# Host-side weight layouts, mask products for the diagonal blocks, eight-group moment steps and unrolled loops in a recommender tower

## The chip, the cores and the metric

One core of one Trainium2 chip runs the whole kernel. The time is device microseconds of that core for one execution. TensorE is written PE (PEld for its weight loads), VectorE DVE, ScalarE ACT, GpSimd POOL, SyncE SP. A measurement of this kernel can tell about one per cent from no change.

## The reference, cut to what matters

The batch is 512 samples. For each, 26 rows of 32 values are gathered, one from each of 26 embedding tables, by a column of `ids`. Two layers of a compressed interaction network follow, and then a small network of three dense layers.

```python
def _cin_layer(x_prev, x0, W, b):
    return jnp.einsum('bik,bjk,hij->bhk', x_prev, x0, W) + b[None, :, None]
...
e = jnp.stack([tbl_0[ids[:, 0]], ..., tbl_25[ids[:, 25]]], axis=1)     # 512 x 26 x 32
x1 = _cin_layer(e, e, W1, b1)                                          # 512 x 128 x 32
x2 = _cin_layer(x1, e, W2, b2)
z = jnp.sum(jnp.concatenate([x1, x2], axis=1), axis=-1)                # 512 x 256
h = jnp.concatenate([z, dense_ctx], axis=1)
h = jnp.maximum(h @ W_top1 + b_top1, 0.0)                              # 512
h = jnp.maximum(h @ W_top2 + b_top2, 0.0)                              # 256
y = h @ W_top3
```

Only sums over the last axis (k) are needed, so the kernel forms products of pairs of fields, multiplies them with the fields over k on TensorE ("moments": every pair with every field, and with a column of ones), and multiplies the moments with weights that are folded from W1 and W2 at the start.

## The kernel before, in words

**Tiles.** The batch is worked in four tiles of 128 samples. Within a tile the 128 samples are 32 groups of 4, and a group's 4 x 32 values of k lie on the 128 partitions.

**Gathers.** POOL issues one indirect DMA for each field and tile, 104 in all (line 242). The fields come in three parts, of 13, 10 and 3 (`PARTS`). There is one buffer `rows` for all tiles: the gathers of part p of tile t+1 wait until part p of tile t has been transposed (`s_turn[p]`). POOL's loop runs twice over two tiles.

**VectorE in a tile.** `half_a` waits until the moments of the tile before are done, transposes part 0 (`fields_in`, line 616) and forms the products of its pairs (`products_a`, lines 771 to 777, 14 instructions). `half_b` transposes parts 1 and 2. `steps` then forms the remaining products four groups at a time (`products_b`, line 788, 8 instructions) and between them copies a few rows of the moments out of PSUM (line 650, four copies for each step).

**ScalarE in a tile.** `fill_diag` (line 467) copies the transposed fields into four diagonal blocks of `diag`, four copies for each part, for the next tile; `copy_moments` takes the moments out of PSUM in eight steps (lines 485 to 489); then come the copies of the first layer's two halves (`z`, lines 495 and 499), and the two dense layers' activations (504, 509) and the output row (514).

**TensorE in a tile.** `moments` (lines 321 and 322) runs 32 groups in eight steps of four, with two pairs of PSUM banks in turn: a step waits for its products and for the evictions of the step two before. The first part of tile t needs `diag` complete. After it come the second dense layer of tile t-1, the sums over the moments (lines 332 to 349) and the first dense layer of tile t.

**Setup.** W1 and W2 are loaded as they are. W2 is transposed on TensorE (line 275) and evicted by ACT (432), W1's pair sums are formed by DVE in small steps (570 to 598), the two are multiplied (281, 287), and DVE adds the parts of `folded` (662). A part of these additions and of the transposes of `folded` stands between the steps of tile 0.

Tiles 1 to 3 run in hardware loops on POOL, PE, ACT and DVE (ACT's covers tiles 1 and 2).

## Time and profile before

| | |
|---|---|
| time, median of 3 runs | 189.18 us (188.01 to 190.05) |
| span of the profiled execution | 269.0 us |
| POOL, gathers | 108.7 us busy, 104 instructions |
| PE, matmuls | 171.1 us busy |
| DVE | 94.1 us busy |
| ACT | 103.7 us busy |

The profiled execution's span is 79.8 us longer than the median of the runs. The profiled execution's own time outside the profiler is not among the times, so its span is all there is of it. The prediction has to say what that difference is.

### The profile page before, as it was taken

Reading aid. Unit: us, or ns where it says so; the run is one execution under the profiler, and the core shown is the slowest. Engines: PE = TensorE matmul, PEld = TensorE weight load, DVE = VectorE, ACT = ScalarE, POOL = GpSimd, SP = SyncE. Lnnn points to the kernel's source line nnn. Section 1 sums busy time; section 2 is a strip of 40 time slices with the busy share of each in tenths; the row PEclk is TensorE's granted clock in tenths of the full one; section 3 lists DMA queues with packets and bytes.
Section 4 is the critical chain, followed back from the end, with each engine's and each line's share of the span. In section 5 each row is a group of like instructions: output and inputs, shape, how many; then the busy total and the mean of one; then the engine's idle time right before and its main releaser. Section 6 shows DMA issues by size and latency. Waiting matters only on the chain.

```text
span 269.0 us, 3544 instructions
## 1 busy us (share of the span) xinstructions
PE 171.1 (64%) x1239; PEld 158.7 (59%) x1239; DVE 94.1 (35%) x370; ACT 103.7 (39%) x267; POOL 109.4 (41%) x110
## 2 busy tenths in 40 slices
PE   7900594209929388986300799954001999899997
PEld 7800583209729287976300789954002999888985
DVE  0576003210943086920000568500003569047200
ACT  1020330019595165494000462951003463966313
POOL 3778777720077400577774003877770000000000
PEclk9975598556997869996555599995555799999999
DMA  6700011000001000011000000001000000000000
GB/s 240 250 12 13 12 14 14 13 7 0 0 10 17 11 1 4 2 12 15 14 12 10 0 0 2 11 12 15 12 12 2 0 0 0 0 0 0 0 0 3
DMA packets 5729, 5.08 MB, mean 19 GB/s; under 512 B 2875, under 2 KB 5061, under 8 KB 5718
## 3 DMA queue, kind: packets, MB, share of 16 engines
q0 software_dynamic: 3328, 1.71, 4.7%
q1 hardware_dynamic: 1698, 2.34, 2.6%
q10 hardware_dynamic: 692, 0.89, 1.0%
q8 instruction: 6, 0.10, 0.2%
q14 instruction: 5, 0.04, 0.1%
HBM read 4.93 MB, written 0.00 MB: 18 GB/s over the span
## 4 chain that ended last, share of the span: by engine, by line
PE 35%; another core or an unknown queue 30%; ACT 15%; DVE 9%; issue 9%; POOL 0%; DVEq 0%; ACTq 0%; POOLq 0%
PE bank L321 9%; ACT diag L467 8%; PE bank L287 4%; DVE t L650 4%; PE bank L322 4%; PE bank L281 4%; PE bank L256 3%; PE bank L332 2%; DVE prod L771 2%; PE bank L372 1%; ACT w2t L432 1%; ACT t L486 1%; DVE prod L616 1%; PE bank L275 1%
## 5 line engine op out<-in xcount | busy, mean ns | idle before, releaser
L242 POOL DMA_INDIRECT rows<-in_tbl_dram,idx x104 | 108.7, 1045 | 91.1 <-DVE prod L616 57.4
L321 PE MATMUL bank<-diag,prod 128*128 128x108 f32 x256 | 60.7, 336 | 56.0 <-DVE t L650 44.3
L321 PEld LDWEIGHTS bank<-diag,prod 128*128 128x128 f32 x256 | 46.6, 227 | 59.5 <-issue 59.5
L650 DVE COPY t<-bank 13x64 f32<-13x64 f32 (+2 forms) x128 | 26.7, 209 | 108.6 <-ACT t L487 66.7
L322 PE MATMUL bank<-diag,prod 128*77 128x64 f32 x256 | 41.7, 249 | 0.3 <-issue 0.3
L322 PEld LDWEIGHTS bank<-diag,prod 128*77 128x77 f32 x256 | 36.8, 173 | 0.5 <-issue 0.5
L485 ACT COPY t<-bank 55x128 f32<-55x128 f32 x32 | 8.3, 259 | 71.9 <-remote 47.8
L467 ACT COPY diag<-prod 32x416 f32<-32x416 f32 (+2 forms) x48 | 33.4, 696 | 1.0
L287 PE MATMUL bank<-w1ab,w2t 128*128 128x169 f32 x52 | 16.0, 489 | 14.6 <-ACT folded L434 9.7
L287 PEld LDWEIGHTS bank<-w1ab,w2t 128*128 128x128 f32 x52 | 12.8, 278 | 17.5 <-ACT folded L434 10.4
L281 PE MATMUL bank<-w1s,w2t 128*128 128x183 f32 x52 | 10.8, 377 | 16.4 <-ACT w2t L432 15.6
L281 PEld LDWEIGHTS bank<-w1s,w2t 128*128 128x128 f32 x52 | 10.3, 233 | 16.9 <-ACT w2t L432 15.8
L788 DVE TENSOR_TENSOR prod<-prod 128x364 f32<-128x364 f32 x32 | 16.5, 536 | 0.8
L489 ACT COPY t<-bank 128x432 f32<-128x432 f32 x32 | 16.4, 512 | 0.0
L434 ACT COPY folded<-bank 128x366 f32<-128x366 f32 x13 | 5.8, 469 | 25.8 <-remote 11.7
L662 DVE TENSOR_TENSOR folded<-folded 128x6 f32<-128x6 f32 (+15 forms) x44 | 5.1, 177 | 27.4 <-ACT folded L434 13.2
L662 DVE TENSOR_TENSOR folded<-folded,ct 128x52 f32<-128x52 f32 (+13 forms) x51 | 11.6, 301 | 7.4 <-ACT ct L437 7.3
L349 PE MATMUL bank<-t,v 128*128 128x128 f32 x104 | 12.7, 279 | 0.0
L332 PE MATMUL bank<-t,v 128*128 128x128 f32 x104 | 12.4, 276 | 0.3 <-ACT t L489 0.3
L332 PEld LDWEIGHTS bank<-t,v 128*128 128x128 f32 x104 | 11.9, 192 | 0.6 <-ACT t L489 0.6
L349 PEld LDWEIGHTS bank<-t,v 128*128 128x128 f32 x104 | 11.9, 192 | 0.5
L363 PE MATMUL bank<-z,wt 128*128 128x128 f32 x64 | 9.0, 286 | 2.8 <-issue 2.1
(79 smaller groups left out, 186.3 us busy)
## 6 DMA issues: line engine op xcount, KB each, us to landing
rows<-in_tbl_dram,idx POOLq DMA_INDIRECT x104
wt<-in_W_top_dram SPq DMA_DIRECT2D x2, 512.0 KB
w<-in_L_rec_W_dram ACTq DMA_DIRECT2D x1, 832.0 KB
w<-in_L_rec_W_dram SPq DMA_DIRECT2D x1, 832.0 KB
w<-in_L_rec_W_dram SPq DMA_DIRECT2D x1, 338.0 KB
idx<-in_ids_dram SPq DMA_DIRECT2D x4, 13.0 KB
vec<-in_L_rec_b_dram ACTq DMA_DIRECT2D x2, 0.5 KB
dctx<-in_dense_ctx_dram ACTq DMA_DIRECT2D x1, 32.0 KB
```

Of the source, the lines that this page charges most:

```text
L242: pool.indirect_dma_start(rows[:, f, :], None, tables[f], bass.IndirectOffsetOnAxis(ap=idx[i][:, f:f + 1], axis=0)).then_inc(s_got[part], 16)
L281: mm = nc.tensor.matmul(ps[:, i * PAIRS:(i + 1) * PAIRS], w2t[:, x0 + i, :], w1s[:], start=True, stop=True)
L287: mm = nc.tensor.matmul(ps[:, i * HALF * HALF:(i + 1) * HALF * HALF], w2t[:, lo + x0 + i, :], rhs, start=True, stop=True)
L321: nc.tensor.matmul(m0[:, g * P:g * P + JW * QUADS], prod[:, G, 0:P], mov, start=True, stop=True)
L322: mm = nc.tensor.matmul(m1[0:M1, g * J1 * QUADS:(g + 1) * J1 * QUADS], prod[:, G, P:P + M1], mov[:, JLOW * QUADS:], start=True, stop=True)
L332: nc.tensor.matmul(Z2[:, 0:P], v0[:, j, :], t0[:, j, :], start=j == HALF, stop=False)
L349: mm = nc.tensor.matmul(Z2[:, 0:P], v0[:, j, :], t0[:, j, :], start=False, stop=j == HALF - 1)
L467: nc.scalar.copy(diag[q, :, f0:f1, r], prod[q, :, col:col + f1 - f0]).then_inc(s_diag, 1)
L489: nc.scalar.copy(dst(t0, 0, P, slice(0, JW)), view(m0, P, slice(0, JW), P)).then_inc(s_e0, 1)
L650: ins = nc.vector.tensor_copy(t1[p0:p0 + HALF, GRAM + slot:GRAM + slot + nb, n].rearrange("p j (g r) -> p j g r", r=QUADS), m1[64:64 + HAL ...
L662: ins = nc.vector.tensor_tensor(dest, dest, term[second], ALU.add)
L788: return eng.tensor_tensor(dst, left, right, ALU.mult)
```

## The change

- **Weights laid out by the host.** The host only reorders and concatenates: W1's two triangles come as two planes `w1p` whose sum is the pair sums, W2 comes transposed (`w2t`), the weights of the first sum come as two planes `w1t`, the vectors as columns, and the dense context transposed and in the order of the groups. The additions stay on the chip: one for `w1s`, one for `z1w`. TensorE's transposes of W2 and of the rest, and their evictions, are gone.
- **Diagonal blocks by mask products.** `fill_diag` on ACT is gone. `fields_in` on DVE multiplies the transposed fields, repeated four times, with a mask `quad` of ones and zeros: one `tensor_tensor` for each part.
- **Moment steps of eight groups.** Four steps for a tile, each with three PSUM banks, two sets in turn; one DVE copy or ACT copy of the small parts covers eight groups, the large one is two copies for each step. `products_b` stays at four groups, but its eight instructions stand in a row, ahead of the copies out of PSUM (`bands`).
- **A row buffer for each tile.** `rows[t]` with semaphores of their own; no gather waits for a transpose.
- **Loops written out.** No hardware loop is left on any engine.
- **Order.** The setup ends before the moments of tile 0 begin; in a tile the sums of `z2` stand ahead of `z1`, and the second dense layer uses one bank and one semaphore.

```diff
-            def fill_diag(t, parts):
-                act.wait_ge(s_mom, t * STEPS + STEPS)
-                for part in parts:
-                    f0, f1, col = PARTS[part]
-                    act.wait_ge(s_turn[part], t + 2)
-                    for r in range(QUADS):
-                        q = slice(32 * r, 32 * r + 32)
-                        nc.scalar.copy(diag[q, :, f0:f1, r], prod[q, :, col:col + f1 - f0]).then_inc(s_diag, 1)
...
             def fields_in(t, part):
                 f0, f1, col = PARTS[part]
-                dve.wait_ge(s_got[part], (t + 1) * (16 * (f1 - f0)))
-                nc.vector.transpose(prod[:, :, col:col + f1 - f0].rearrange("p g f -> p f g"),
-                                    rows[:, f0:f1, :]).then_inc(s_turn[part], 1)
+                n = f1 - f0
+                dve.wait_ge(s_got[t][part], 16 * n)
+                nc.vector.transpose(prod[:, :, col:col + n].rearrange("p g f -> p f g"),
+                                    rows[t][:, f0:f1, :]).then_inc(s_turn[part], 1)
+                dve.wait_ge(s_turn[part], t + 1)
+                nc.vector.tensor_tensor(diag[:, :, f0:f1, :],
+                                        with_dims(prod[:, 0, col:col + 1], (PCOLS, GROUPS), (1, n), (0, QUADS)),
+                                        with_dims(quad[:, 0:1], (0, GROUPS), (0, n), (1, QUADS)), ALU.mult)
...
-            with nc.gpsimd.Fori(0, TILES // 2) as u:
-                for i in range(2):
-                    pool.wait_ge(s_idx[i], u * 16 + 16)
-                    for part, (f0, f1, _) in enumerate(PARTS):
-                        pool.wait_ge(s_turn[part], u * 2 + i + 1)
+            for t in range(TILES):
+                if t < 2:
+                    pool.wait_ge(s_idx[t], 16)
+                for part, (f0, f1, _) in enumerate(PARTS):
...
-                for s in range(STEPS + 2):
-                    if s < STEPS:
-                        products_b(nc.vector, prod, s * GSTEP, GSTEP).then_inc(s_pb, 1)
-                    if between and 2 <= s < STEPS:
-                        add(*between[s - 2])
-                    if s >= 2:
-                        m1 = MOM[s % 2][1]
...
+                for s in range(PRODS):
+                    products_b(nc.vector, prod, s * GPROD, GPROD).then_inc(s_pb, 1)
+
+            def bands(t):
+                if t:
+                    dve.wait_ge(s_z1, t)
+                for s in range(STEPS):
+                    m1 = bank[3 * (s % 2) + 2]
+                    dve.wait_ge(s_mom, t * STEPS + s + 1)
```

How the instructions stand. DVE at the start of a tile after the first, before: L616 transposes part 0 out of `rows`, L771 are the pair products.

```order
L615 ISA [waits s_mom]
L616 STREAM_TRANSPOSE prod<-rows 128x13x32 [waits s_got0]
L622 REGISTER_ALU
L771 TENSOR_TENSOR prod<-prod 128x32x5 [waits s_turn0]
L771 TENSOR_TENSOR prod<-prod 128x32x4
L771 TENSOR_TENSOR prod<-prod 128x32x3
```

The same place in the changed kernel, tile 1:

```order
L447 STREAM_TRANSPOSE prod<-rows 128x13x32 [waits s_got1_0,s_mom]
L450 TENSOR_TENSOR diag<-prod,quad 128x32x52 [waits s_turn0]
L599 TENSOR_TENSOR prod<-prod 128x32x5
L599 TENSOR_TENSOR prod<-prod 128x32x4
L599 TENSOR_TENSOR prod<-prod 128x32x3
```

A product with 1,664 elements on each partition, with two inputs in SBUF, has come in directly ahead of the 14 products.

DVE from part 1 to the second step's copies, before:

```order
L616 STREAM_TRANSPOSE prod<-rows 128x10x32 [waits s_got1]
L628 COPY prod<-prod 128x32x6 [waits s_turn1]
L615 REGISTER_ALU
L616 STREAM_TRANSPOSE prod<-rows 128x3x32 [waits s_got2]
L788 TENSOR_TENSOR prod<-prod 128x4x91 [waits s_dup,s_turn2]
L788 TENSOR_TENSOR prod<-prod 128x4x91 x2
L644 REGISTER_ALU
L645 REGISTER_ALU [waits s_mom]
L647 ISA [waits s_e1]
L650 COPY t<-bank 13x4x16 [waits s_z]
```

And in the changed kernel:

```order
L447 STREAM_TRANSPOSE prod<-rows 128x10x32 [waits s_got1_1]
L450 TENSOR_TENSOR diag<-prod,quad 128x32x40 [waits s_turn1]
L462 COPY prod<-prod 128x32x6
L447 STREAM_TRANSPOSE prod<-rows 128x3x32 [waits s_got1_2]
L450 TENSOR_TENSOR diag<-prod,quad 128x32x12 [waits s_turn2]
L616 TENSOR_TENSOR prod<-prod 128x4x91 [waits s_dup]
L616 TENSOR_TENSOR prod<-prod 128x4x91 x7
L477 COPY t<-bank 13x4x32 [waits s_mom,s_z1]
```

One mask product and eight pair products now stand in a row without a wait between them; before it was three, and then one at a time between copies out of PSUM.

POOL's gathers, before (one round of the loop, two tiles):

```order
L242 DMA rows<-in_tbl_dram,idx 128x32 [waits s_turn0]
L242 DMA rows<-in_tbl_dram,idx 128x32 x12
L242 DMA rows<-in_tbl_dram,idx 128x32 [waits s_turn1]
L242 DMA rows<-in_tbl_dram,idx 128x32 x9
L242 DMA rows<-in_tbl_dram,idx 128x32 [waits s_turn2]
L242 DMA rows<-in_tbl_dram,idx 128x32 x2
```

In the changed kernel:

```order
L197 DMA rows<-in_tbl_dram,idx 128x32 [waits s_idx0]
L197 DMA rows<-in_tbl_dram,idx 128x32 x25
L197 DMA rows<-in_tbl_dram,idx 128x32 [waits s_idx1]
L197 DMA rows<-in_tbl_dram,idx 128x32 x77
```

The waits for the transposes are gone; only the index tables are waited for.

## Rows read from the trace of the kernel before

**Rows 1.** The page: span, and the chain that ended last, by engine.

```profile
span 269.0 us, 3544 instructions
...
PE 35%; another core or an unknown queue 30%; ACT 15%; DVE 9%; issue 9%; POOL 0%; DVEq 0%; ACTq 0%; POOLq 0%
```

**Rows 2.** The chain in order of time, its long waits: start us, us, what.

```profile
44.74 6.55 issue
...
126.92 20.83 another core or an unknown queue
...
183.90 21.32 another core or an unknown queue
```

**Rows 3.** Timeline of POOL and ACT at the end of the first of the two longest.

```profile
143.61 0.94 POOL L242 DMA_INDIRECT rows<-in_tbl_dram,idx  x1 [0.30 <-issue]
147.85 0.26 ACT L485 COPY t<-bank 55x128 f32<-55x128 f32 x1 [20.70 <-remote]
```

**Rows 4.** All gathers as a group: count, busy us, mean ns, idle before.

```profile
L242 POOL DMA_INDIRECT rows<-in_tbl_dram,idx x104 | 108.7, 1045 | 91.1 <-DVE prod L616 57.4 <-issue 33.7
```

**Rows 5.** Timeline of POOL and DVE, 4 to 29 us.

```profile
4.55 1.14 POOL L242 DMA_INDIRECT rows<-in_tbl_dram,idx  x1 [3.17 <-issue]
...
19.88 0.95 POOL L242 DMA_INDIRECT rows<-in_tbl_dram,idx  x1 [0.30 <-issue]
...
22.26 0.88 DVE L616 STREAM_TRANSPOSE prod<-rows 128x416 f32<-128x416 f32 x1 [2.03 <-DMA rows<-in_tbl_dram,idx]
...
23.17 2.19 DVE L771 TENSOR_TENSOR prod<-prod 128x160 f32<-128x160 f32 x11
23.63 0.95 POOL L242 DMA_INDIRECT rows<-in_tbl_dram,idx  x1 [0.30 <-issue]
24.88 3.34 POOL L242 DMA_INDIRECT rows<-in_tbl_dram,idx  x1 [0.30 <-issue]
25.29 1.15 DVE L773 TENSOR_TENSOR prod<-prod 128x960 f32<-128x960 f32 x1
26.35 1.05 DVE L777 TENSOR_TENSOR prod<-prod 128x384 f32<-128x384 f32 x2
```

**Rows 6.** The same engines in tiles 1 and 2.

```profile
111.38 3.00 POOL L242 DMA_INDIRECT rows<-in_tbl_dram,idx  x1 [0.30 <-issue]
...
114.79 1.43 DVE L788 TENSOR_TENSOR prod<-prod 128x364 f32<-128x364 f32 x3
115.93 1.11 POOL L242 DMA_INDIRECT rows<-in_tbl_dram,idx  x1 [0.30 <-issue]
...
165.46 4.26 POOL L242 DMA_INDIRECT rows<-in_tbl_dram,idx  x1 [20.91 <-DVE prod L616]
```

**Rows 7.** A one-input DVE instruction beside gathers.

```profile
14.94 2.94 DVE L604 MEMSET diag<- 128x3456 f32 x1 [0.65 <-issue]
16.13 0.95 POOL L242 DMA_INDIRECT rows<-in_tbl_dram,idx  x1 [0.30 <-issue]
```

**Rows 8.** Timeline of the last tile, without gathers beside it.

```profile
227.50 0.34 DVE L616 STREAM_TRANSPOSE prod<-rows 128x96 f32<-128x96 f32 x1
...
234.12 1.50 ACT L467 COPY diag<-prod 32x96 f32<-32x96 f32 x4
...
244.44 0.43 PE L321 MATMUL bank<-diag,prod 128*128 128x108 f32 x2
...
245.60 0.42 PE L321 MATMUL bank<-diag,prod 128*128 128x108 f32 x2
...
249.49 2.00 PE L372 MATMUL bank<-h,wt 128*128 128x128 f32 x16
```

**Rows 9.** The chain: first matmul of the last tile's moments.

```profile
235.75 0.47 PE bank L321 x2
```

**Rows 10.** Groups of the last tile by shape: DVE products.

```profile
L788 DVE TENSOR_TENSOR prod<-prod 128x364 f32<-128x364 f32 x8 | 4.1, 536 | 0.2
...
L773 DVE TENSOR_TENSOR prod<-prod 128x960 f32<-128x960 f32 x1 | 1.2, 1166 | 0.0
```

More of the change, by code:

```diff
@@ L78 @@
 M1 = 64 + HALF
+CROSS = HALF * HALF
 GRAM = J1 // 2
@@ L96, with dlrm_tower @@
 MT2 = N_TOP2 // P
-def dlrm_tower(nc, dense_ctx, ids, tables, W_top1, b_top1, W_top2, b_top2, W_top3, W1, b1, W2, b2, out):
+RING = 8
+SETUP = [("fold", j, 2) for j in range(0, FIELDS, 2)]
+SETUP += [("ctA", x, min(3, HALF - x)) for x in range(0, HALF, 3)]
+SETUP += [("ctB", x, min(3, HALF - x)) for x in range(0, HALF, 3)]
+SETUP += [("v0", j, min(4, FIELDS - j)) for j in range(HALF, FIELDS, 4)]
+SETUP += [("v1", x, min(4, J1 - 1 - x)) for x in range(0, J1 - 1, 4)]
+SETUP += [("v0", j, min(4, HALF - j)) for j in range(0, HALF, 4)]
+DONE = {kind: q + 1 for q, (kind, first, n) in enumerate(SETUP)}
+FOLD_A = 1 + SETUP.index(("fold", HALF - 1, 2))
+def dlrm_tower(nc, io, tables, out):
     with ExitStack() as ctx:
@@ L323, in moments, with z2_low @@
+                        mm = nc.tensor.matmul(m1[0:M1, a1:a1 + J1 * QUADS], prod[:, G, P:P + M1],
                                               mov[:, JLOW * QUADS:], start=True, stop=True)
                     mm.then_inc(s_mom, 1)
-                    if s < len(between):
-                        make(between[s])
-            def z2_b(t):
-                pe.wait_ge(s_e0, t * STEPS + STEPS)
+            def z2_low():
+                for j in range(HALF):
+                    nc.tensor.matmul(Z2[:, 0:P], v0[:, j, :], t0[:, j, :], start=j == 0, stop=False)
@@ new lines, in layer1 @@
+                    nc.tensor.matmul(L1[m][:, 0:P], wt1c[:, chunk(m)], dctx[:, t * P:(t + 1) * P], start=True, stop=False)
+                for m in range(MT1):
+                    nc.tensor.matmul(L1[m][:, 0:P], wt1[:, 1, chunk(m)], z[1][:], start=False, stop=False)
+                pe.wait_ge(s_z1s, t + 1)
+                for m in range(MT1):
+                    mm = nc.tensor.matmul(L1[m][:, 0:P], wt1[:, 0, chunk(m)], z[0][:], start=False, stop=True)
+                    mm.then_inc(s_l1, 1)
@@ L383, in _ @@
                 make(q)
-            pe.wait_ge(s_sf, ring)
+            pe.wait_ge(s_sf, len(SETUP))
             pe.wait_ge(s_pad, 1)
-            moments(0, range(before, done["v1"]))
-            for q in range(done["v1"], done["v1"] + 2):
-                make(q)
-            z2_b(0)
-            z1(0)
-            for q in range(done["v1"] + 2, len(setup)):
-                make(q)
-            z2_second_chunk()
-            pe.wait_ge(s_sf, len(setup))
-            z2_a()
+            pe.wait_ge(s_vec, 32)
@@ L518, in _ @@
+            for q in range(len(SETUP)):
                 take(q)
-            act.wait_ge(s_pad, 1)
-            fill_diag(0, [0])
-            for q in range(done["fold"], ring):
-                take(q)
-            fill_diag(0, [1, 2])
-            for q in range(ring, before):
-                take(q)
-            copy_moments(0, range(before, done["v1"]))
-            for q in range(done["v1"], len(setup)):
-                take(q)
-            fill_diag(1, [0])
-            copy_z1(0)
-            fill_diag(1, [1])
@@ L605, in _ @@
+            link(nc.vector.memset(diag[:, :, ONE, :], 0.0))
+            link(nc.vector.memset(v1[32:64, :, :], 0.0))
+            linked()
+            for r in range(QUADS):
+                nc.vector.memset(quad[32 * r:32 * r + 32, r:r + 1], 1.0)
+                link(nc.vector.memset(diag[32 * r:32 * r + 32, :, ONE, r], 1.0))
+            dve.wait_ge(s_w1p, 16)
+            nc.vector.tensor_tensor(w1s[:], w1p[:, 0, :], w1p[:, 1, :], ALU.add).then_inc(s_w1s, 1)
             link(nc.vector.memset(t1[:, GRAM:GRAM + GSLOTS, :], 0.0))
@@ L676, in _ @@
             add(cross, 1, True)
-            half_b(0)
-            cross = cross_b(folded, ct[1])
-            dve.wait_ge(s_sf, done["ctB"])
-            third = -(-len(cross) // 3)
-            steps(0, [(cross[x * third:(x + 1) * third], second, second == 1 and x == 2)
-                      for second in range(2) for x in range(3)])
-            with nc.vector.Fori(1, TILES) as t:
+            half_a(0)
+            dve.wait_ge(s_sf, DONE["ctB"])
+            cross = cross_b(folded, ct[1])
+            add(cross, 0, False)
+            add(cross, 1, True)
+            half_b(0)
+            bands(0)
+            for t in range(1, TILES):
                 half_a(t)
                 half_b(t)
-                steps(t)
+                bands(t)
 def with_dims(ap, *dims):
@@ L811 @@
+    out = nc.dram_tensor("out_0_dram", (BATCH, 1), F32, kind="ExternalOutput").ap()
+    dlrm_tower(nc, aps, [aps[f"tbl_{i}"] for i in range(FIELDS)], out)
     r = _run(nc, [arrays], core_ids=[0])
```

515 lines of the change are left out of this document (219 added, 296 removed).

## The prediction

> **What bounds the kernel now.** I read four views: the page's chain by engine, the chain in order of time, the timeline of POOL and DVE, and the groups of the gathers.
>
> The first thing to settle is that the span is 269.0 us [rows 1] and the timed median 189.18. The chain gives 30% of the span, 80 us, to "another core or an unknown queue" [rows 1], and the long pieces of it stand beside gathers: ACT does nothing from 127 until 147.85, that is 3.3 us after the last gather of that tile has ended (143.61 + 0.94) [rows 3]. Adding the wait at 44.74, which stands in the same kind of stretch [rows 2], gives 86.6 us. I take these waits as a thing of the profiled execution that the timed ones don't have, since nothing else makes room for the 79.8 us between them.
>
> Without them, what is last? The reader should look at POOL. A gather takes 0.95 us and the next starts 0.30 us after its end, so one every 1.25 us [rows 5]. All 104 are 108.7 us busy and 33.7 us in the small gaps (3.2 of them ahead of the first) [rows 4, 5]. POOL waited 57.4 us for transposes [rows 4], but only because those came late, behind the waits above: once the engines run freely, the transposes of tile t come well before POOL has finished tile t+1's earlier parts. So POOL runs without a break, and its last gather ends at 4.55 + 108.7 + 30.5 = 143.8. Behind it: 1.4 us until DVE sees it (the 13th gather ends at 20.83, DVE starts at 22.26 [rows 5]); the transpose of part 2 (0.34) and ACT's four diagonal copies (1.50) [rows 8] with their gaps, 2.2; the moments, 235.75 to 249.49 [rows 8, 9], 13.7; and 249.49 to the end at 269.0, 19.5 [rows 1, 8]. The sum is 180.6 us of span. The median is 8.6 above it, which I keep as what lies around the span; it is the one fitted number, and the same kernel start and end stand in both kernels.
>
> The compute engines' own chain is not far from that: the span less the 86.6 us of such waits leaves 182.4. So both chains are close, and which leads decides what the change is worth.
>
> **Why the gathers are not simply 104 x 1.25 us.** Alone, 104 gathers would be busy 98.8 us; they are busy 108.7 [rows 4]. The 9.9 us sit in a few of them: 3.34, 3.00 and 4.26 us instead of 0.95 [rows 5, 6]. Each lies beside DVE's run of pair products and ends 0.8 us after that run (26.35 + 1.05 = 27.40; 24.88 + 3.34 = 28.22) [rows 5]. Three products in a row cost the gather at 115.93 0.16 us [rows 6], while a memset of 2.94 us costs the gather at 16.13 nothing [rows 7]. So a DVE product with two inputs in SBUF holds the gather back, and a row of them without a gap can hold it until the row ends. Not always: the gather at 23.63 passed through line 771's products unharmed [rows 5].
>
> The Trainium skill ("SBUF — State Buffer", Who interferes with whom) has the shared port as a lock held for one whole instruction, and infers that `tensor_tensor` does not stall descriptor generation. The first rule would let a gather wait for at most the 1.15 us product that it meets, the second for nothing; the 2.4 us that the gather at 24.88 lost [rows 5] is more than either. By the first, a gather caught by the mask product would lose 1.9 instead of 1.15 us, 0.75 a tile, and the whole forecast would be about 190.
>
> **The change part by part.**
>
> *Row buffers.* They remove POOL's 57.4 us of waits [rows 4], which by the argument above are not there in a timed run. Price 0. If the waits were real, the profile's span would have to be the timed one.
>
> *Mask products.* ACT loses twelve copies a tile, of which only part 2's 1.50 us lie on the path. DVE gains three products. From 364 elements in 536 ns and 960 in 1166 ns [rows 10] an element costs 1.06 ns, so 1,664, 1,280 and 384 elements take 1.9, 1.5 and 0.56 us. In the last tile, part 1 lands 3.75 us before part 2, so its 1.5 is covered; the path from part 2 to the first matmul is 0.34 + 0.56 + one pair product 0.54 + gaps, 1.6 instead of 2.2: -0.6.
>
> *Eight-group steps, products ahead.* A group of moments takes 0.387 us on PE when nothing holds it (three from 244.44 to 245.60 [rows 8]), 32 take 12.4; before they took 13.7 since DVE's copies and products alternated. -1.3. The tail behind the moments has the same matmuls in another order: the eviction of the last eight groups and the wait of both second-layer activations for one bank lengthen it, the earlier copy of `z`'s second half shortens it. I take +0.1, and 1 either way in the range.
>
> *What the same edits do to the gathers.* Each tile's first row of products (23.17 to 27.40 [rows 5]) grows from 4.2 us to 6.1 by the mask product ahead of it: a gather that is caught waits up to 1.9 longer. Part 1's product of 1.5 us is new: 0 to 1.5, I take 0.5, as gathers are sometimes let through. Eight pair products and the small mask product now stand in a row, 0.56 + 8 x 0.45 = 4.1 us (three take 1.43, the last of them 0.54 [rows 6, 10]), where before there were three and then single ones between copies from PSUM: 0 to 4.1, I take 1.3, nearer to the 0.16 of three in a row than to the row's length. That is 3.7 us for each of tiles 0 to 2; in tile 3 only the first two still meet gathers, 2.4. The sum is 13.5. Its bounds: nothing, if DVE never delays a gather in a timed run; (1.9 + 1.5 + 4.1) x 3 + 3.4 = 26, if every row catches one fully.
>
> *Setup.* About 40 TensorE transposes and 11 evictions go; in exchange the moments of tile 0 wait for all of `folded`, whose additions stand in two long rows. The 52nd gather, tile 1's last, can't end before 4.55 + 52 x 1.25 = 69.6, and I take the setup and tile 0 to be done by then, so that while the gathers lead the setup has no price. Without that cover I put it at -8 to 0, and take -3 in rival B. The longer rows of additions can hold gathers too: 0 to 3, in the range only.
>
> *Loops.* The Trainium skill ("Runtime: NRT & Kernel Launch", Instruction fetch mechanics) says that a taken branch breaks the sequential prefetch and stalls. ACT's 20.8 us at 126.92 is behind such a branch [rows 2], but the 6.55 us at 44.74 [rows 2] is in straight code, and both stand beside gathers. By that rule the change would give back up to what the loops really cost; it is a reason for the second rival, and in my sum it is 0.
>
> **The sum.** The last gather ends at 143.8 + 13.5 = 157.3. Then 1.4 + 1.6 + 12.4 + 19.6 = 35.0. Span 192.3, and 8.6 around it: **200.9 us**, 6% slower. With the bounds of the gather term alone 187.4 to 213; since rows let gathers through, its own range is 192 to 208.
>
> **The rivals.**
>
> *A. The gathers lead, but DVE's longer rows don't hold them back more.* For it: gathers pass unharmed at 23.63 [rows 5]. Against it: the three that lost 2.0 to 3.3 us [rows 5, 6]. It gives 189.2 - 0.6 - 1.3 + 0.1 = 187.4; with 0.75 us a tile about 190. It decides from a gather term below 4 us.
>
> *B. The engines lead, and the change speeds them up.* For it: 182.4 against 180.6, the setup is shorter, and a tile is shorter by 1.3 on PE and free of ACT's diagonal copies. The engine chain of 182.4 loses 1.3 in each of four tiles, about 1.4 more in each of three gaps between tiles (1.50 of the diagonal copies [rows 8]), and some 3 in the setup: 170.0. The gathers, even with none held back, end at 4.55 + 104 x 1.25 - 0.3 = 134.3, and 35.0 behind that is 169.3, just under it. If the engines led before, 189.2 - 182.4 = 6.8 lies around the span: 176.8; with half of the gathers' excess of before, about 182. It needs timed runs in which the gathers are neither held back nor what the before waits for.
>
> *C. A wait of the profiled kind is in timed runs as well,* in small; then unbroken gathering makes it worse than my sum. Above 208.
>
> **How the numbers follow.** Chances: forecast 0.53, A 0.20, B 0.22, C 0.05. Predicted is the forecast's time, 200.9. The range of 8 in 10 must reach into A and B: 178 to 208 leaves out part of B, C and little else. Within 1% (187.3 to 191.1), which is about what a measurement of this kernel can tell from no change, lie more than half of A and a little of the forecast's lower end: 0.15. Faster: B and the rest of A, 0.28. Slower: 0.57.
>
> **What the changed profile would show.** Gathers from 4.5 us on without a wait for DVE; their mean above 1045 ns, with several of 2 to 6 us beside lines 450, 601 to 605 and 616 (the forecast), or at most as many as before (A, B). PE idle ahead of the last tile's moments, released by DVE behind a gather (forecast, A), or not idle (B). The moments of a tile with full supply in 12.4 us. The span itself may be far above the timed run, as before. I would be wrong if timed gathers come faster than one in 1.25 us, or if what lies around the span is 15 us and not 8.6: both make the engines lead.

## The result, and the profile of the changed kernel

The changed kernel takes 199.81 us (median of 4 runs, 197.00 to 200.54), the kernel before 188.68 (4 runs, 188.01 to 190.05): a ratio of 1.055, 95% interval 1.042 to 1.068, so slower. (The ratio is taken over the quicker executions of each kernel; the two medians as they stand give 1.059.) The profiled execution is the one of 200.54 us.

One thing has to be known before any further number is read. The kernel *before*, which took 189 us beside the changed one, took 264 to 284 us on each of the four chips that ran the experiments below, timed and not only profiled; its profile of 269.0 us of span is of that kind too. I call these chips "stopping" and the one of the recorded pair "free"; what stops is shown with the experiments. Which chip the recorded pair ran on is not known, so it is not shown that the difference lies in the chip and not in something else that was different at that time.

The page of the changed kernel, beside [rows 1] and [rows 4] (in the slices each digit is a 40th of the span):

```profile
span 198.8 us, 3020 instructions
...
POOL 4787778988777887877778877777797730000000
...
POOL 62%; PE 16%; issue 16%; DMA 2%; DVE 1%; POOLq 1%; ACT 0%
...
L197 POOL DMA_INDIRECT rows<-in_tbl_dram,idx x104 | 126.4, 1215 | 32.9 <-issue 31.4
L250 PE MATMUL bank<-diag,prod 128*128 128x108 f32 x256 | 58.9, 332 | 24.3 <-DVE prod L616 23.7
```

The share of "another core or an unknown queue" is gone from the chain; in its place POOL's gathers are 62% of it, and nearly all of the 16% of "issue" are the 0.30 us between them. POOL never waits for DVE (57.4 us before [rows 4]), and yet the gathers are busy for 126.4 us where they were for 108.7: a mean of 1215 ns for 1045. An unhindered gather takes about 0.947, so 104 of them 98.5, and 27.9 us are lost. All but some 1.0 us of that stands beside the rows of DVE that follow here; and where the same kernel ran with DVE nearly at rest beside the gathers (the changed kernel in experiment 5), the same 104 were busy for 98.6 us:

```profile
L197 POOL DMA_INDIRECT rows<-in_tbl_dram,idx x104 | 98.6, 949 | 32.9 <-issue 31.4
```

In the recorded run the gathers' row of digits is unbroken for the first 32 of 40 slices. PE waits 23.7 us for pair products at the start of three tiles' moments: it is the engine that is fed too slowly.

POOL and DVE over part 0 of tile 2, and the eight pair products of tile 1 (the timeline, beside [rows 5, 6]):

```profile
87.10 3.67 DVE L616 TENSOR_TENSOR prod<-prod 128x364 f32<-128x364 f32 x8
87.58 1.32 POOL L197 DMA_INDIRECT rows<-in_tbl_dram,idx  x1 [0.30 <-issue]
89.20 1.04 POOL L197 DMA_INDIRECT rows<-in_tbl_dram,idx  x1 [0.30 <-issue]
...
105.33 1.89 DVE L450 TENSOR_TENSOR diag<-prod,quad 128x1664 f32<-128x1664 f32 x1
105.61 2.43 POOL L197 DMA_INDIRECT rows<-in_tbl_dram,idx  x1 [0.30 <-issue]
107.14 2.16 DVE L599 TENSOR_TENSOR prod<-prod 128x160 f32<-128x160 f32 x11
108.35 3.81 POOL L197 DMA_INDIRECT rows<-in_tbl_dram,idx  x1 [0.30 <-issue]
```

The mask product of line 450 ends at 107.22, the gather beside it at 108.04, 0.82 later; the next one lasts to 112.16. The eight products in a row, 3.67 us long, cost their gathers only 0.37, 0.09 and, another gather on, 0.09 us.

In tile 0 the additions of the setup stand in the same stretch. POOL's pieces of the chain there:

```profile
28.97 1.95 POOL rows L197
31.22 2.17 POOL rows L197
33.70 2.43 POOL rows L197
36.43 4.53 POOL rows L197
41.26 1.99 POOL rows L197
43.55 2.44 POOL rows L197
46.30 1.86 POOL rows L197
```

Unhindered, each would be 0.95. These seven lose 10.7 us; with the products behind them tile 0 loses 11.1. Tiles 1 and 2 lose 5.6 each, and tile 3 loses 4.9: its eight products come after the last gather and meet none.

The end of the chain, and the windows of the last tile (us, then busy us of PE, PEld, DVE, ACT, POOL, then granted clock, DMA share, GB/s), beside [rows 8]:

```profile
158.98 3.09 DMA rows<-in_tbl_dram,idx
...
163.62 0.74 PE bank L250 x2
```

```profile
163.60:169.30 5.70, 5.68 (x32) 5.70 (x33) 3.01 (x7) 0.00 (x0) 0.00 (x0) 0.52 0.00 0
169.30:178.00 8.70, 8.70 (x93) 8.70 (x92) 3.16 (x12) 5.14 (x15) 0.00 (x0) 1.00 0.01 2
```

The last gather is issued at 158.98 and ends at 160.68. PE, idle for 7.62 us before it, starts the moments of the last tile at 163.62 with a granted clock of 0.52, the lower of its two levels, and keeps it for the first eight groups: 5.7 us, where eight groups at the full clock take 3.1 (8 x 0.387, from [rows 8]). The moments take 14.9 us, not 12.4.

### The profile page after: what moved, and what is told of

Its sections match the earlier page's. It is cut to its first block, busy times and chain, and to the rows that moved or that the text cites. A ratio compares the mean times of both kernels' runs of the same rounds, so it can differ in the third digit from the quotient of the medians.

```text
span 198.8 us, 3020 instructions
## 1 busy us (share of the span) xinstructions
PE 154.1 (78%) x1193; PEld 148.3 (75%) x1193; DVE 91.8 (46%) x293; ACT 57.0 (29%) x156; POOL 127.1 (64%) x110
## 4 chain that ended last, share of the span: by engine, by line
POOL 62%; PE 16%; issue 16%; DMA 2%; DVE 1%; POOLq 1%; ACT 0%
POOL rows L197 62%; PE bank L250 5%; PE bank L251 2%; PE bank L294 2%; PE bank L257 2%; PE bank L261 2%; DMA rows<-in_tbl_dram,idx 2%; PE bank L264 1%; DMA idx<-in_ids_dram 1%; POOLq L97 1%; PE bank L301 1%; PE bank L283 1%; PE bank L281 1%; PE bank L270 0%; PE bank L286 0%
## 5 line engine op out<-in xcount | busy, mean ns | idle before, releaser
L197 POOL DMA_INDIRECT rows<-in_tbl_dram,idx x104 | 126.4, 1215 | 32.9 <-issue 31.4
L250 PE MATMUL bank<-diag,prod 128*128 128x108 f32 x256 | 58.9, 332 | 24.3 <-DVE prod L616 23.7
L250 PEld LDWEIGHTS bank<-diag,prod 128*128 128x128 f32 x256 | 46.1, 226 | 25.2 <-issue 24.2
L477 DVE COPY t<-bank 13x128 f32<-13x128 f32 (+1 forms) x64 | 16.8, 263 | 36.0 <-PE bank L251 35.3
L369 ACT COPY t<-bank 55x256 f32<-55x256 f32 (+2 forms) x48 | 14.1, 294 | 62.2 <-PE bank L251 61.8
L447 DVE STREAM_TRANSPOSE prod<-rows 128x416 f32<-128x416 f32 (+2 forms) x12 | 7.8, 654 | 33.5 <-DMA rows<-in_tbl_dram,idx 33.5
L450 DVE TENSOR_TENSOR diag<-prod,quad 128x1664 f32<-128x1664 f32 (+2 forms) x12 | 15.8, 1314 | 0.4
L257 PE MATMUL bank<-t,v 128*128 128x128 f32 x104 | 14.2, 300 | 1.8 <-ACT t L377 1.8
L616 DVE TENSOR_TENSOR prod<-prod 128x364 f32<-128x364 f32 x32 | 14.7, 532 | 0.0
L228 PE MATMUL bank<-ident,folded 128*128 128x128 f32 x26 | 6.0, 422 | 10.8 <-DVE folded L488 10.8
L228 PEld LDWEIGHTS bank<-ident,folded 128*128 128x128 f32 x26 | 5.3, 225 | 11.2 <-issue 11.2
L261 PE MATMUL bank<-t,v 128*128 128x128 f32 x104 | 12.8, 281 | 0.0
```

The lines of the kernel that those rows point to most:

```text
L197: pool.indirect_dma_start(rows[t][:, f, :], None, tables[f], bass.IndirectOffsetOnAxis(ap=idx[:, t, f:f + 1], axis=0)).then_inc(s_got[t][p ...
L250: nc.tensor.matmul(m0[:, a0:a0 + JW * QUADS], prod[:, G, 0:P], mov, start=True, stop=True)
L257: nc.tensor.matmul(Z2[:, 0:P], v0[:, j, :], t0[:, j, :], start=j == 0, stop=False)
L261: nc.tensor.matmul(Z2[:, 0:P], v0[:, j, :], t0[:, j, :], start=False, stop=False)
L369: return nc.scalar.copy(dst, src)
L450: nc.vector.tensor_tensor(diag[:, :, f0:f1, :], with_dims(prod[:, 0, col:col + 1], (PCOLS, GROUPS), (1, n), (0, QUADS)), with_dims(quad[:, ...
```

## The experiments

Every kernel was compared with the kernel before on its own chip. The times are medians with the range of all runs.

### 1. The kernel before with its loops written out

```diff
-            with nc.gpsimd.Fori(0, TILES // 2) as u:
+            for u in range(0, TILES // 2):
...
-            with nc.tensor.Fori(1, TILES) as t:
+            for t in range(1, TILES):
...
-            with nc.scalar.Fori(1, TILES - 1) as t:
+            for t in range(1, TILES - 1):
...
-            with nc.vector.Fori(1, TILES) as t:
+            for t in range(1, TILES):
```

> The kernel before with its loops written out and nothing else. Theory (gathers lead and are held back by DVE's rows of two-input products): 187 to 190 us, as before, since the loops lie beside the gathers; the gathers run without a break and, having lost some 15 us to DVE's rows, end near 150. Rival (loop branches cost time in timed runs): 180 to 185. For the profile: if the 80 us of waits for an unknown queue belong to the hardware loops, this span lies near the timed run; if they belong to gathers beside engine work under the profiler, it is near 269 again.

Measured: 274.72 us (269.28 to 277.48), the kernel before on the same chip 273.76 (271.27 to 283.81). The kernel before did not take 189 there: this chip is of the stopping kind. Since that chip's spread is wide, the same kernel ran again on another with more runs.

> The kernel before with its loops written out, a second time, since the first fell on a chip on which the kernel before takes 274 us and not 189, so that it doesn't speak to the recorded pair. If this one has the kernel before near 189: theory (gathers lead) 187 to 190 us, the last gather ending near 150, with some 15 us of excess over 0.95 us each, part by part beside DVE's two-input products; rival (loop branches cost time) 180 to 185. If the kernel before is again near 274: again no difference.

Measured: 267.90 us (10 runs, 265.09 to 270.85) against 269.44 (13 runs, 265.88 to 272.94): 0.995, interval 0.990 to 1.001. The page of the first of the two runs still has the gaps:

```profile
PE 38%; another core or an unknown queue 33%; ACT 18%; issue 6%; DVE 4%; POOL 0%; DVEq 0%; ACTq 0%; POOLq 0%
```

There is no loop left, and 33% of the chain is still the nameless wait (20% in the second run, where "issue" has 15%). So the waits of [rows 2] are not the price of a branch, and the term of 0 for the loops stands, on chips of this kind; on a free one it was not run.

### 2. The mask products undone: ACT fills the diagonal blocks in the changed kernel

```diff
+            def fill_diag(t, parts):
+                if t:
+                    act.wait_ge(s_mom, t * STEPS)
...
+                    for r in range(QUADS):
+                        q = slice(32 * r, 32 * r + 32)
+                        nc.scalar.copy(diag[q, :, f0:f1, r], prod[q, :, col:col + f1 - f0]).then_inc(s_diag, 1)
...
-                nc.vector.tensor_tensor(diag[:, :, f0:f1, :], ...
```

> The changed kernel with the diagonal blocks filled by ACT copies again, as before, instead of DVE's mask products. Theory: the mask products stand in the rows of line 450 and 599 to 605 that hold gathers for 2.4 + 3.8 us in each of tiles 1 to 3 and for about 0.75 beside part 1; without them some 10 us of the gathers' excess of 27.9 go, and the time is 188 to 193. Rival (DVE's work is itself the chain, 3.9 us more for each tile): the four tiles get 16 us back on DVE but ACT's 8.5 for each tile stand in their place, 195 to 200.

Measured: 328.68 us (327.27 to 329.45), 1.205 of before on that chip (1.196 to 1.214).

> The changed kernel with ACT's diagonal copies instead of the mask products, a second time, for the same reason. With the kernel before near 189: theory 188 to 193, some 10 us less gather excess than the 27.9 of the changed kernel; rival (DVE's chain leads) 195 to 200. With the kernel before near 274: above 320, as the first time.

Measured on a second chip: 326.87 (326.59 to 329.27), 1.222 (1.210 to 1.233). As a test of what the mask products cost the gathers it tells nothing: the gathers lost 0.3 us in all, but so they did in every changed kernel with unbroken gathers on these chips (0.6 in experiment 3), mask products or not, since DVE hardly ran beside them. What it does show, on such chips, is what the mask products are for. Behind the gathers the engines lead, and there PE waited 32.3 us in four waits of up to 8.9 us for ACT's fills of the one `diag` buffer. Against the changed kernel on a third chip (286.98, experiment 5) it is some 40 us slower, 1.20 to 1.22 against 1.063 of before. (It also fills `diag` with zeros as a whole in the setup, and lets ACT start the fills of the next tile only when the moments of the tile before are done.)

### 3. Four of the eight pair products moved back between the copies from PSUM

```diff
-                for s in range(PRODS):
+                for s in range(4):
...
+                    if s < 2:
+                        for x in (4 + 2 * s, 5 + 2 * s):
+                            products_b(nc.vector, prod, x * GPROD, GPROD).then_inc(s_pb, 1)
```

> The changed kernel with four of a tile's eight pair products (products_b) moved behind the PSUM copies of steps 0 and 1. Theory: the row of eight costs gathers only some 0.5 us a tile, so 198 to 200, no change that can be told. Rival (the row of eight is what holds the gathers, up to 4 us a tile): 190 or less.

Measured: 290.03 us (287.47 to 290.58), 1.061 of before (1.051 to 1.071). It doesn't tell the theories apart either, for the same reason; that the row of eight costs a gather little is read from the rows of the changed kernel above. But its trace is the clearest of what stops. Three windows (busy us and count of PE, PEld, DVE, ACT, POOL; clock, DMA share, GB/s): with the gathers, the 15 us behind the last of them, and the rest. After them the first window in the trace of the recorded changed kernel, and then some rows of this run's timeline inside the first window (in brackets is the idle time before an instruction; "issue" is idle time for which the view shows no cause, and "remote" puts it on nothing in this core):

```profile
16.00:133.00 117.00, 25.73 (x82) 18.19 (x81) 5.64 (x44) 6.48 (x14) 88.59 (x94) 0.54 0.08 13
133.40:148.70 15.30, 3.28 (x7) 1.72 (x6) 0.00 (x0) 0.58 (x1) 0.00 (x0) 0.50 0.00 1
148.80:288.00 139.20, 120.54 (x1041) 115.63 (x1041) 82.99 (x231) 47.66 (x139) 0.00 (x0) 0.91 0.00 1
```

```profile
16.00:133.00 117.00, 87.66 (x660) 84.83 (x659) 65.82 (x218) 36.09 (x96) 93.84 (x77) 0.84 0.08 12
```

```profile
106.15 0.95 POOL L197 DMA_INDIRECT rows<-in_tbl_dram,idx  x1 [0.30 <-issue]
106.22 0.44 PE L222 MATMUL bank<-w1s,w2t 128*128 128x169 f32 x1 [2.35 <-issue]
...
109.03 0.44 PE L222 MATMUL bank<-w1s,w2t 128*128 128x169 f32 x1 [2.37 <-issue]
...
110.44 0.58 ACT L344 COPY ct<-bank 128x507 f32<-128x507 f32 x1 [17.04 <-remote]
...
112.51 0.17 DVE L491 TENSOR_TENSOR folded<-folded 128x8 f32<-128x8 f32 x1 [1.93 <-issue]
113.91 0.17 DVE L491 TENSOR_TENSOR folded<-folded 128x6 f32<-128x6 f32 x1 [1.23 <-issue]
```

In 117 us PE gets 82 matmuls done and ACT 14 copies, while POOL issues 94 gathers at their usual pace, 0.95 + 0.30 us. In the same 117 us of the recorded run PE does 660 and ACT 96. PE's matmuls come one in 2.8 us with no wait that the view can name; DVE's additions of 0.17 us come 1.4 us apart. The stop outlasts the gathers: the last one ends at 133.36, and in the 15.3 us behind it PE still does only 7 matmuls, though POOL issues nothing any more and the DMA share is 0.00. Then 1041 matmuls run in 139 us. In the kernel before, with its rows of 26 gathers, ACT came back 3.3 us after the last gather ([rows 3]). What works itself off in that time is not shown.

### 4. The changed kernel, and the kernel before, without gathers

Each part's rows come by one plain DMA from fixed rows of two tables, 12 DMAs in place of 104; the lookup is left out.

```diff
-                    for f in range(f0, f1):
-                        pool.indirect_dma_start(
-                            rows[t][:, f, :], None, tables[f],
-                            bass.IndirectOffsetOnAxis(ap=idx[:, t, f:f + 1], axis=0)).then_inc(s_got[t][part], 16)
+                    pool.dma_start(rows[t][:, f0:f1, :],
+                                   tables[3 + 2 * (t % 2)][0:P * (f1 - f0), :].rearrange("(p f) e -> p f e", p=P)
+                                   ).then_inc(s_got[t][part], 16)
```

> The changed kernel with each part's rows loaded by one plain DMA from fixed rows of two tables instead of 26 indirect DMAs a tile; it leaves the lookup by index out. Theory (gathers lead): the engines' own chain shows, 160 to 172 us, and PE has no wait ahead of a tile's moments longer than 1 us. Rival (the engines lead and the mask products lengthened their chain): 195 or more.

Measured: 167.11 us (166.50 to 167.16), 0.612 of before (0.608 to 0.616).

> The kernel before with its lookups replaced by one plain DMA for each part of a tile, from fixed rows of two tables; the lookup is left out. It measures the engines' own chain of before, as the same edit did for the changed kernel (165.4 of span, 167.1 timed). Theory (in the recorded pair the kernel before was led by its gathers, or close to it): its engines' chain is long too, near the 182.4 that its profile leaves without the waits of the profiled kind; I take 172 to 180, timed. If it comes below 168, the change did not shorten the engines' chain at all and all of the 11 us between the recorded times are the gathers' doing plus nothing given back; if it comes above 185, the engines led before and my gather chain of 180.6 was beside the point. On a chip where gathers stop the engines, no such stops may show here: the span is that of free engines.

Measured: 172.86 us (6 runs, 170.88 to 173.14), 0.641 of before (0.638 to 0.644) on another chip. The two chains, the changed kernel first, and of each the window up to tile 0's first moments:

```profile
PE 75%; DVE 13%; DMA 6%; ACT 2%; SPq 1%; issue 1%; DVEq 0%
```

```profile
0.00:49.40 49.40, 33.47 (x194) 32.47 (x194) 30.65 (x136) 19.01 (x40) 7.21 (x18) 0.84 0.34 117
```

```profile
PE 44%; ACT 21%; DVE 18%; issue 11%; DMA 4%; SPq 1%; DVEq 0%; ACTq 0%
```

```profile
0.00:41.80 41.80, 33.81 (x211) 30.39 (x211) 27.82 (x139) 27.49 (x52) 4.06 (x12) 1.00 0.30 98
```

No nameless wait is left in either, and with it goes the stopping: it belongs to the gathers, not to the rest of the kernel. Whether it is their being indirect or their number was not tested; 104 small plain DMAs were not run. The engines' own chain is 169.5 us of span before and 165.4 after. Both recorded times are well above these, 188.7 and 199.8 against 172.9 and 167.1: with the gathers in, the kernel before takes 15.8 us more and the changed one 32.7. For the changed kernel its own trace shows that the gathers lead on the free chip; for the kernel before this is an inference, as it has no trace from there. By these numbers the change speeds the engines up by 5.8 us timed and loses 16.9 to the gathers. (All of these differences compare runs on different chips.)

Inside the chain the 4.1 us of span are a gain and a loss. From tile 1 to tile 2 the moments start 27.24 us apart instead of 29.97:

```profile
78.42 0.37 PE L249 MATMUL bank<-diag,prod 128*128 128x108 f32 x2
...
105.66 0.37 PE L249 MATMUL bank<-diag,prod 128*128 128x108 f32 x2
```

```profile
76.30 0.47 PE L320 MATMUL bank<-diag,prod 128*128 128x108 f32 x2 [0.31 <-ACT diag L466]
...
106.27 0.47 PE L320 MATMUL bank<-diag,prod 128*128 128x108 f32 x2 [0.31 <-ACT diag L466]
```

but the moments of tile 0 start 7.6 us later, at 49.4 instead of 41.8. PE waits 10.6 us for DVE's additions to `folded` there, and takes up work at a mean granted clock of 0.84 in that window where before had 1.00.

### 5. The waits for a row buffer put back into the changed kernel

First the changed kernel itself on a stopping chip, beside the variant with POOL's waits.

> The changed kernel itself beside the kernel before on one chip. If the kernel before takes about 270 us there (two chips so far), the engines hardly move while gathers are issued, so an unbroken 130 us of gathers is paid nearly in full ahead of some 150 us of engine work: 285 to 292, and about 3 us for each tile above the variant with the products apart, at most. If the kernel before takes about 189: 197 to 201, as recorded.

Measured: 286.98 us (282.24 to 290.70), before on the same chip 269.97 (264.52 to 271.62): 1.063 by the medians.

```diff
                 for part, (f0, f1, _) in enumerate(PARTS):
+                    if t:
+                        pool.wait_ge(s_turn[part], t)
                     for f in range(f0, f1):
```

> The changed kernel with the waits of the row buffers put back: the gathers of a part wait until that part of the tile before has been transposed. Theory where the kernel before takes about 270 us: the breaks in the gathers let the engines run, as they did in the kernel before, so 250 to 272, at least 15 us less than without the waits. Rival: the breaks only push the gathers back, 290 or more. Where the kernel before takes about 189: the waits cost nothing, since the transposes are done long before POOL gets there, 198 to 201.

Measured: 251.78 us (250.43 to 252.75), 0.933 of before by the medians and 35 us below the changed kernel (32 us by the lowest time of each). PE and POOL in 40 slices, of the changed kernel on this chip and of the variant, and POOL's wait in the second:

```profile
PE   8591311111111111111144169799999999999996
...
POOL 5777777777777777773000000000000000000000
```

```profile
PE   7598427381794226899523399996331899999995
...
POOL 5777760059877750687777303977775000000000
```

```profile
POOL rows L199 <- DVE prod L449: 39.6, 3, 16.4
```

With unbroken gathers PE is at a tenth of its time in 15 of the 19 slices of 7.2 us in which they run. With 39.6 us of pauses in POOL, PE fills up in each pause and in the first part of each row of gathers. On such a chip the row buffer for each tile, the part of the change that I priced at 0, costs more than everything else in it brings.

### 6. What holds a gather: one-input masks, and masks issued twice

All on one chip, on the basis of experiment 5, where DVE runs beside gathers.

> The changed kernel with the row-buffer waits put back, again, on another chip and beside the two variants of it. If the chip stops the engines behind long runs of gathers: 0.93 of before, about 250. If it does not: the gathers lead and each wait of POOL for the transposes costs; POOL waits for the parts of tile t-1 only where these are late, which I put at 0 to 6 us above the changed kernel, 200 to 206.

Measured: 252.03 us (251.47 to 253.48), 0.934 of before (0.929 to 0.940); the gathers lose 20.5 us in all.

```diff
-                nc.vector.tensor_tensor(diag[:, :, f0:f1, :],
-                                        with_dims(prod[:, 0, col:col + 1], (PCOLS, GROUPS), (1, n), (0, QUADS)),
-                                        with_dims(quad[:, 0:1], (0, GROUPS), (0, n), (1, QUADS)), ALU.mult)
+                for r in range(QUADS):
+                    nc.vector.tensor_scalar(diag[:, :, f0:f1, r], prod[:, :, col:col + n], quad[:, r:r + 1], None, ALU.mult)
```

> As a_rowwait_2, with each mask product as four products by a column of the mask (one input in SBUF and a scalar for each partition, a fourth of the elements each) in place of one with two inputs. Theory (only the two-input products hold a gather, until their row ends): the gather beside the small and large mask product loses only what the pair products behind it take, so the 3.8 us gathers of tiles 2 and 3 fall to 2.9 or less, the gather of 1.87 beside part 1's mask to about 0.95, excess of all gathers down by 1.2 to 2 us a tile, 5 to 8 in all, and the time by 2 to 6. Rival (DVE's strided writes or any DVE work hold gathers, whatever the number of inputs): the same durations as in a_rowwait, 1.87 and 3.8, and the time within 1%.

Measured: 248.56 us (247.49 to 250.47), 0.922 of before (0.916 to 0.929); the gathers lose 25.2 us.

```diff
+        spare = [sb(f"spare{i}", [P, GROUPS, FIELDS, QUADS]) for i in range(2)]
...
+                nc.vector.tensor_tensor(spare[t % 2][:, :, f0:f1, :],
+                                        with_dims(prod[:, 0, col:col + 1], (PCOLS, GROUPS), (1, n), (0, QUADS)),
+                                        with_dims(quad[:, 0:1], (0, GROUPS), (0, n), (1, QUADS)), ALU.mult)
```

> As a_rowwait_2, with every mask product issued twice, the second into a tile that nobody reads. Theory (a gather is held until the row of two-input products ends): the gather beside part 0's row loses the whole added 1.9 us (3.80 becomes 5.7), the one beside part 1's mask 1.3 to 1.5 more (1.87 becomes 3.2 to 3.4), and the excess grows by about 3.3 us a tile, 10 to 14 in all. DVE itself is 3.8 us busier a tile. Time 4 to 14 above a_rowwait_2. Rival (a gather waits for at most one instruction): no gather is longer than about 3.8, and the excess grows by less than 1 us a tile.

Measured: 251.76 us (250.46 to 252.34), 0.931 of before (0.926 to 0.936); the gathers lose 22.5 us.

The timelines of tile 2, DVE and POOL, in the order base, masks twice, one-input masks:

```profile
102.61 1.89 DVE L452 TENSOR_TENSOR diag<-prod,quad 128x1664 f32<-128x1664 f32 x1
102.84 2.48 POOL L199 DMA_INDIRECT rows<-in_tbl_dram,idx  x1 [10.15 <-DVE prod L449]
105.62 3.81 POOL L199 DMA_INDIRECT rows<-in_tbl_dram,idx  x1 [0.30 <-issue]
...
111.73 3.66 DVE L618 TENSOR_TENSOR prod<-prod 128x364 f32<-128x364 f32 x8
111.91 1.16 POOL L199 DMA_INDIRECT rows<-in_tbl_dram,idx  x1 [0.30 <-issue]
```

```profile
105.35 1.88 DVE L456 TENSOR_TENSOR spare<-prod,quad 128x1664 f32<-128x1664 f32 x1
106.56 1.50 POOL L200 DMA_INDIRECT rows<-in_tbl_dram,idx  x1 [0.30 <-issue]
108.36 3.79 POOL L200 DMA_INDIRECT rows<-in_tbl_dram,idx  x1 [0.30 <-issue]
```

```profile
101.30 1.74 POOL L199 DMA_INDIRECT rows<-in_tbl_dram,idx  x1 [5.86 <-DVE prod L449]
103.34 4.41 POOL L199 DMA_INDIRECT rows<-in_tbl_dram,idx  x1 [0.30 <-issue]
...
110.24 3.68 DVE L617 TENSOR_TENSOR prod<-prod 128x364 f32<-128x364 f32 x8
110.91 3.83 POOL L199 DMA_INDIRECT rows<-in_tbl_dram,idx  x1 [0.30 <-issue]
```

Twice the masks cost 2.0 us of gather time, not 10 to 14: my theory that a gather stays caught until the whole row ends fell for the large products. The gather beside the first mask is let go between the two (2.48, as in the base), the next waits for the rest of the second (1.50), and the 3.8 beside the pair products stays 3.8. So of two mask products back to back each holds one gather, 0.8 us past its own end.

The one-input masks held the gathers beside them for less (2.48 became 1.74, and beside part 1's mask 1.87 became 1.28), but not for nothing, as the theory had it: 1.28 is still above 0.95. And the sum rose by 4.7 us, where a fall of 5 to 8 was expected; no gather fell from 3.8 to 2.9. The gather behind them now begins 0.6 us after the pair products, not 1.2, and lasts 4.41 us to their end; and the gather that begins 0.67 us after the row of eight (110.91 against 110.24) is held for the whole of it, 3.83 us, where the base's, begun 0.18 us after it, lost 0.2. Whether a row of short products lets a gather through or keeps it to its end depends on a few tenths of a microsecond in how the two are phased. Its time is 1.4% under the base all the same, with 34.4 us of POOL's waits for 40.0; on a stopping chip more or fewer gather microseconds are not what sets the time.

The variant with one-input masks is the quickest measured version that does the whole computation on a stopping chip. It and its base were not run on a free one, where POOL leads and pauses would be paid for.

## Why the prediction was right, and where it was not

**The number.** Forecast 200.9 us; the measured median is 199.81 and the profiled execution took 200.54. That the gathers lead and lose more to DVE than they did in the profile of before is what the trace shows. That the sum came within about 1 us is in good part luck: several terms were off and cancelled, above all 6.9 us too much around the span against 4.2 too little in the gathers and 2.5 too little in the last tile's moments (the measured column is of the profiled execution and ends each term at a row of the chain):

| term | forecast | measured |
|---|---|---|
| start of the first gather | 4.55 | 2.93 |
| gathers busy | 108.7 + 13.5 = 122.2 | 126.4 |
| gaps between them | 30.5 | 31.35 |
| last gather to the first matmul | 1.4 + 1.6 = 3.0 | 1.42 + 1.52 = 2.94 |
| moments of the last tile | 12.4 | 14.94 |
| the rest | 19.6 | 20.24 |
| around the span | 8.6 | 1.74 |
| sum | 200.85 | 200.54 |

**"A thing of the profiled execution that the timed ones don't have".** This step failed. The nameless waits of [rows 2] are real time of real runs, on chips of the stopping kind: timed runs of the kernel before take 264 to 284 there. The recorded pair didn't have them, so taking them out of the sum came out right, for a wrong reason.

**"8.6 above it, which I keep as what lies around the span".** Failed as well: 200.54 less 198.8 is 1.7. The other 6.9 us of before were somewhere in its span. If its chain had the form that I gave it, its last gather ended at about 188.7 - 1.7 - 36.8 = 150, not 143.8, and its gathers lost about 16 us to DVE, not the 9.9 that the profile of a stopping chip shows. That fits what the experiments show (DVE hardly runs beside gathers there, so it can't hold them), but no trace of the kernel before from a free chip was to be had: it is an inference. If it holds, the fitted constant carried a loss of the gathers into the sum under another name, and that is why the total came out.

**The gather term, 13.5.** Measured losses are 27.9 us against the forecast's 9.9 + 13.5 = 23.4; against the inferred 16 of before the increase is some 12. By its pieces: the first row of part 0, forecast 1.9 for the mask on top of what the pair products took, loses 1.5 beside the mask and 2.9 beside the products a tile (2.43 and 3.81 less 0.95). That the caught gather is let go between mask and products, and another is caught, was not foreseen; the sum hardly changes. Part 1's mask, forecast 0.5, costs 0.75. The row of eight pair products, forecast 1.3, costs 0.55; experiment 6 shows that it can be 2.9 with another phase, so 1.3 was in the middle of a term that is decided by tenths of a microsecond. The setup's additions, "0 to 3, in the range only", are what was missed: tile 0 loses 11.1 against 5.6 in tiles 1 and 2, so by that comparison they cost some 5.5.

The rule that I weighed against it, in the Trainium skill ("SBUF — State Buffer", Who interferes with whom), is half borne out: a large product does hold a gather for that one instruction, as a lock held for an instruction would. But against what the section infers, a gather is held beside `tensor_tensor`, and a row of short ones can hold one gather for 3.8 us.

**Moments, -1.3 a tile.** Right where the supply is full: in the two traces of experiment 4 the moments of tile 2 last 12.3 us (105.66 to 117.93) in the changed kernel and 13.8 (106.27 to 120.09) in the kernel before. In the recorded run it was lost again, since PE idles for 7.6 us before the last tile and then runs eight groups at half clock, 2.6 us. A term for the clock was missing in the sum.

**Setup, 0 while the gathers lead, -3 in rival B.** The sign was wrong: tile 0's moments start 7.6 us later, because they now wait for all of `folded`. That is in the runs without gathers; in the recorded run it is hidden behind the gathers, and it ate most of what B hoped for.

**Row buffers, 0.** Right on the free chip as far as it can be told. In the recorded trace of the changed kernel each transpose that a gather would have waited for ends 12.9 us or more ahead of that gather (the nearest is part 0 of tile 0: transposed at 33.38, the gather starts at 46.30), so the old waits would have cost nothing there; the variant with them was not run there. On a stopping chip the same edit costs 35 us (experiment 5).

**Loops, 0.** Shown for the kernel before on a stopping chip (0.990 to 1.001); on a free one, and in the changed kernel, it was not run.

**Rival A** needed gathers that lose no more than before; 27.9 us of losses against 9.9 shown or 16 inferred speak against it, and the time does. **Rival B** had the engines leading both kernels; they led neither, at 172.9 and 167.1 timed. Its price of the tiles, 2.7 us each, was right (29.97 - 27.24); its start from 182.4 was not, for a stopped stretch holds more than its named waits. **Rival C** describes the other chips: there unbroken gathers do make it worse, 1.063 of before at 287 us.

**What stays open:** what it is that lets these gathers stop the other engines on some chips, whether the kernel before lost its 15.8 us in the way that is inferred here, and how much of the 11.1 us between the recorded times each part of the change has: no experiment ran on a chip where it could be measured. The split above is read from the changed kernel's own trace and from the two kernels without gathers.

## What to carry to other kernels

Before a wait is dropped from a profile as not real, or a constant is fitted to close the gap to the timed median, look for the row that it would have; a fitted constant hides a term, and here, as far as can be told, it was right only by what it hid. Where one engine issues many indirect DMAs, a two-input DVE product that is "free" beside them is paid for on the issuing engine, so price work by whom it stands beside, and remember that an engine fed more slowly also comes back at a lower clock. Taking away a wait that only seems to pace an engine can take away the pauses in which all the others run: leave the pauses in until a run shows that they cost something.

## What the runs showed of the hardware

- On four chips, rows of 26 to 104 gathers (128 rows of a table each, one in 1.25 us) bring the other engines nearly to rest, mostly some 13 to 18 us after the first. In the first row of the kernel before it comes and goes: 48 matmuls still run at their usual pace from 29.9 to 39.8 us, 25 us after the first gather. Behind rows of 26 the engines come back 3.3 us after the last gather has ended [rows 3]; behind 104 in a row only after 15 us (experiment 3). While it lasts a matmul comes in 2.8 us, DVE's short instructions in 1.4 us (some in 0.7), and a copy on ACT waits 17 to 21 us. Twelve plain DMAs of the same bytes do nothing of the kind. The same kernel took 189 us in the recorded pair and 270 on the four chips.
- A gather that meets one large two-input product of DVE ends 0.8 us after that product. Two such products back to back, of 1.9 us each, hold one gather apiece; a row of eight of 0.45 us lets gathers pass with 0.1 to 0.4 us of delay, or keeps one for 3.8 us; the one let through began 0.2 us after the row's start, the one kept 0.7 us after it.
- One-input products that write the same elements hold a gather for less, but longer than the 0.95 us that it takes alone: 1.74 for 2.48 us, 1.28 for 1.87.
- The time of a run is 1.7 to 2.0 us above its span, in every kernel here.
